# Two graph-attention layers in fp8 and bf16: products that read the weights' three parts in place

## The reference

```python
def _L0_gnn_ref(h, adj, a):
    src, dst = h @ a[:D, 0], h @ a[D:, 0]
    e = src[:, None] + dst[None, :]
    e = jnp.where(e > 0, e, 0.01 * e)
    e = jnp.where(adj > 0, e, NEG_INF)
    return jax.nn.softmax(e, axis=1) @ h
...
x = _layernorm(x + _L0_gnn_ref(x, adj, L0_gnn_a), axis=-1)
x = _layernorm(x + _L1_gnn_ref(x, adj, L1_gnn_W, L1_gnn_a), axis=-1)
```

## Time and profile before

| | |
|---|---|
| Median of 3 runs | 437.58 us (437.0 to 438.23) |
| The profiled execution's own time | 437.87 us |
| Its span, first to last instruction | 436.0 us |
| Mean granted TensorE clock | 0.992 |
| Busy: TensorE, weight loads | 406.4, 397.8 us |
| Busy: VectorE, ScalarE, GpSimd | 380.3, 382.9, 252.2 us |
| Chain that ended last | TensorE 75%, VectorE 15%, issue 6% |

### The profile page before, as it was taken

The page is one execution under the profiler, slowest core; times in us unless marked ns, Lnnn a source line. Parts: engine busy times, 40 slices in busy tenths (PEclk is TensorE's granted clock), DMA queues, the critical chain, the costliest instruction groups (busy, mean ns, idle before and its releaser), DMA issues.

```text
span 436.0 us, 11844 instructions
## 1 busy us (share of the span) xinstructions
PE 406.4 (93%) x4484; PEld 397.8 (91%) x4484; DVE 380.3 (87%) x683; ACT 382.9 (88%) x590; POOL 252.2 (58%) x292
## 2 busy tenths in 40 slices
PE   1599999999999999999999999999999999999980
PEld 1388999999999999999998998999999999999980
DVE  4799998899898989999889997689999999999963
ACT  3899986979979799779998989999999999999930
POOL 5533353753738547296493135568696969695931
PEclk9999999999999999999999999999999999999996
DMA  5999989799897998988610000000000000000000
GB/s 118 99 107 108 90 75 98 68 101 80 78 102 66 95 85 73 90 73 88 83 52 1 2 26 2 2 26 2 27 2 26 0 24 1 24 2 26 2 26 17
DMA packets 22766, 22.48 MB, mean 52 GB/s; under 512 B 1344, under 2 KB 22464, under 8 KB 22720
## 3 DMA queue, kind: packets, MB, share of 16 engines
q0 software_dynamic: 17424, 16.78, 44.4%
q1 hardware_dynamic: 4208, 4.05, 2.9%
q10 hardware_dynamic: 1088, 1.05, 0.7%
HBM read 69.30 MB, written 2.10 MB: 164 GB/s over the span
## 4 chain that ended last, share of the span: by engine, by line
PE 75%; DVE 15%; issue 6%; POOL 1%; DMA 1%; ACT 0%; DVEq 0%; POOLq 0%
PE acc L1223 67%; PE tb L1147 5%; DVE neg L831 3%; DVE pos L842 3%; DVE mask_t L757 2%; PE srcb L1157 1%; DMA mask_t<-in_x 1%; DVE split L814 1%; DVE mask_t L814 1%; PE pg L1191 1%; DVE scr L857 1%; DVE wmov L820 1%; DVE mask_t L913 1%; DVE dcol L921 1%; DVE enc L814 1%
## 5 line engine op out<-in xcount | busy, mean ns | idle before, releaser
L670 ACT ACTIVATE neg<-srcb,dcol 128x512 int8<-128x512 f32 x512 | 358.2, 973 | 4.4 <-PE acc L1223 4.0
L1223 PE MATMUL acc<-wmov,pos 128*128 128x195 bf16 x2016 | 357.1, 248 | 3.6 <-DVE pos L842 2.6
L1223 PE MATMUL acc<-wmov,neg 128*128 128x195 bf16 x2016 | 357.3, 249 | 0.0
L1223 PEld LDWEIGHTS acc<-wmov,pos 128*128 128x128 fp8e4 x2016 | 198.5, 98 | 7.6 <-DVE pos L842 5.6
L1223 PEld LDWEIGHTS acc<-wmov,neg 128*128 128x128 fp8e4 x2016 | 197.5, 98 | 2.3 <-issue 1.3
L842 DVE TENSOR_TENSOR pos<-neg,mask_t 128x1024 uint16<-128x1024 uint16 x128 | 104.8, 819 | 15.3 <-DVE neg L831 1.6
L831 DVE TENSOR_TENSOR neg<-neg,mask_t 128x1024 uint16<-128x1024 uint16 x128 | 102.9, 804 | 10.8 <-ACT neg L670 8.0
L490 POOL DMA_DIRECT2D enc<-in_adj x31 | 24.7, 798 | 63.5 <-DVE scr L857 31.1
L757 DVE TENSOR_SCALAR mask_t<-tb 128x512 uint32<-128x512 uint32 (+1 forms) x64 | 43.9, 686 | 6.7 <-PE tb L1147 6.0
L1147 PE MATMUL tb<-ident,enc 128*128 128x128 f32 x256 | 39.5, 278 | 2.7 <-DMA enc<-in_adj 2.7
L742 DVE SCALAR_TENSOR_TENSOR odd<-mask_t,odd 128x1024 uint32<-128x1024 uint32 x32 | 38.8, 1213 | 0.0
(11 more groups left out here) (139 smaller groups left out, 301.7 us busy)
## 6 DMA issues: line engine op xcount, KB each, us to landing
enc<-in_adj POOLq DMA_DIRECT2D x31, 512.0 KB, 8.2
mask_t<-in_x ACTq DMA_DIRECT2D x4, 256.0 KB, 5.7
x_rows<-xout SPq DMA_DIRECT2D x8, 128.0 KB, 3.1
resid<-x_rows SPq DMA_DIRECT2D x8, 128.0 KB, 2.1
out<-xout SPq DMA_DIRECT2D x8, 128.0 KB, 1.7
wmov<-mask_t SPq DMA_DIRECT2D x2, 390.0 KB, 3.4
enc<-in_adj POOLq DMA_DIRECT2D x2, 256.0 KB, 8.3
resid<-in_a SPq DMA_DIRECT2D x1, 64.0 KB, 4.6
```

Of the source, the lines that this page charges most:

```text
L670: ins = nc.scalar.activation(neg[:, k % SR, :, b], srcb[:, q % 2, :], ACT.Sign, bias=dcol[:, layer, c:c + 1])
L1223: ins = nc.tensor.matmul(acc[t][:, side * WC:(side + 1) * WC], m[:, t * P:(t + 1) * P, b], wmov[:, c, side * WC:(side + 1) * WC], start=fi ...
```

## The change

Every group gets a home of its own, 1,040 fp32 words: pairs of words (product, rest), side by side for each column. As bf16 these are four halves a column: the lower half of the product, its upper half, the lower half of the rest, its upper half. VectorE's second subtraction writes the rounded third part over the lower half of the rest, so halves 1, 2 and 3 of four are the three parts, and the moving operand reads them there, `halves_of(layer, g)[:, b, side, :, 1:4]`. `wmov`, `split`, the staged words, `keep_parts` and `move_weights` go. The accumulators hold the parts of a column side by side, 65 times 3, and the sums read them so. Layer 0's groups 0 and 1 lie in the mask's last supertile, the others in `wts`; layer 1's groups lie in `apart_wts`, in lots of `enc_lots` (the adjacency buffer, 16 words longer a lot) and in the first three lots of `wts`. Their writers wait for those homes to be free.

```diff
+        def home(layer, g):
+            if layer == 0 and g < TAIL:
+                flat = last_words[:, first_tail + g * LOT:first_tail + (g + 1) * LOT]
+            elif layer == 0:
+                flat = wts[:, g - TAIL]
+            else:
+                flat = {0: apart_wts[:, :], 1: enc_lots[:, 0], 2: enc_lots[:, 1], 3: wts[:, 0], 4: wts[:, 1],
+                        5: wts[:, 2], 6: enc_lots[:, 2], 7: enc_lots[:, 3]}[g]
+            return flat
+        def wait_for_home(eng, g):
+            if g in (1, 2, 6, 7):
+                lot = {1: 0, 2: 1, 6: 2, 7: 3}[g]
+                eng.wait_ge(turned, KB * (NQ - 1) + KP * (lot + 1))
+            elif g:
+                eng.wait_ge(mm_done, KB * (NQ - 1) + g)
+        def parts_of(layer, g):
+            return home(layer, g).rearrange("p (b s c r) -> p b s c r", b=NB, s=2, r=2)
+        def halves_of(layer, g):
+            return home(layer, g).bitcast(BF16).rearrange("p (b s c h) -> p b s c h", b=NB, s=2, h=4)
+        def moving(layer, g, b, side):
+            return halves_of(layer, g)[:, b, side, :, 1:4]
...
 def multiply(eng, ops, layer, g):
-            if n > 1:
-                eng.wait_ge(w_vec, WEIGH * (n - 1))
-                eng.wait_ge(w_act, n - 1)
-            ops.tensor_tensor(parts_of(layer, g)[:, :, :, 0, :], ...
+            ops.tensor_tensor(parts_of(layer, g)[:, :, :, :, 0], ...
...
 gpsimd, layer 0, supertile 6:
-                    groups = {3: (0,), 5: (1,)}
+                    groups = {3: (0,), 7: (1,)}
 gpsimd, change_layers:
-                w = wmov[:, NB * 7:NB * 8].rearrange("p b (s c) -> p b s c", s=2)[:, :, :, 0:2 * FD]
-                pool.wait_ge(w_vec, WEIGH * (NQ + 7) + 1)
-                nc.gpsimd.tensor_copy(w, top_of(1, 7).rearrange("p b s r c -> p b s (r c)")).then_inc(w_pool, 1)
...
 scalar:
-                nc.scalar.copy(w, top_of(layer, g).rearrange("p b s r c -> p b s (r c)")).then_inc(w_act, 1)
...
 extract, last supertile of layer 0:
-                            dve.wait_ge(moved[g], 16)
+                            dve.wait_ge(mm_done, KB * (NQ - 1) + g + 1)
...
 weigh:
-                nc.vector.tensor_tensor(rest, both[:, :, :, 0, :], top[:, :, :, 0, :], ALU.subtract)\
+                nc.vector.tensor_tensor(rest, product, halves[:, :, :, :, 1], ALU.subtract).then_inc(w_vec, 1)
-                nc.vector.tensor_tensor(w[:, :, :, 2, :], rest, top[:, :, :, 1, :], ALU.subtract)\
+                nc.vector.tensor_tensor(halves[:, :, :, :, 2], rest, halves[:, :, :, :, 3], ALU.subtract)\
...
 vector, layer 0, supertile 7:
+                        if k == 2:
+                            weigh(1, 1)
-                        if k >= STAGED + 2:
+                        if k >= 4:
                             weigh(1, k - 2)
 vector, layer 0, supertile 6:
-                        if k in (4, 6):
-                            weigh(1, k // 2 - 2)
+                        if k == 5:
+                            weigh(1, 0)
...
 tensor, products and one_tile:
-                                acc[t][:, side * WC:(side + 1) * WC], m[:, t * P:(t + 1) * P, b],
-                                wmov[:, c, side * WC:(side + 1) * WC], start=first, stop=last, skip_group_check=True)
+                                acc[t][:, side * WC:(side + 1) * WC].rearrange("p (c r) -> p c r", r=SPLIT),
+                            m[:, t * P:(t + 1) * P, b],
+                                moving(layer, k, b, side), start=first, stop=last, skip_group_check=True)
```

More of the change, by code:

```diff
@@ L31 @@
 EARLY = 5
-STAGED = 2
+TAIL = 2
+LOT = NB * 2 * FD * 2
 LOOKS = (4, 5, 6)
@@ L86, in fast_attention @@
         ident = sb("ident", [P, P], F32)
-        ones = sb("ones", [P, 1], F32)
-        share = sb("share", [P, 1], F32)
+        single = sb("single", [P, 3], F32)
+        ones, share, strange = (single[:, i:i + 1] for i in range(3))
         att1 = sb("att1", [F, 2], F32)
@@ L167, in fast_attention @@
         a_set = sem("a_set")
-        w_prod = [sem(f"w_prod{i}") for i in range(2)]
+        w_prod = sem("w_prod")
         w_vec = sem("w_vec")
-        w_act = sem("w_act")
-        w_pool = sem("w_pool")
         limits = sem("limits")
@@ L236, in weights_of @@
[L236 to L248, removed]
+        first_tail = KB * TI * P - TAIL * LOT
@@ L685, in body @@
                             exps_of_d(0, 0, KB * NB, 0)
-                        else:
-                            keep_parts(0, k - 1)
                         if k == 6:
                             exps_of_s(0, 0, 2)
-                    if layer == 0 and is_second(q) and k == 0:
-                        keep_parts(0, KB - 1)
                     if layer == 0 and is_second(q) and k == KB - 1:
@@ L748, in extract @@
                 if is_last(q):
-                    if k == 0:
-                        dve.wait_ge(w_act, NQ + STAGED)
-                    for g in range(STAGED):
-                        if k == steps_of(g)[0]:
-                            dve.wait_ge(moved[g], 16)
+                    for g in range(TAIL):
+                        if k == (first_tail + g * LOT) // (TI * P):
+                            dve.wait_ge(mm_done, KB * (NQ - 1) + g + 1)
                 apart(dve, q)
@@ L808, in weigh @@
                 n = NQ * layer + g
-                both, top = parts_of(layer, g), top_of(layer, g)
-                rest = both[:, :, :, 1, :]
-                w = weights_of(layer, g).rearrange("p b (s r c) -> p b s r c", s=2, r=SPLIT)
-                dve.wait_ge(w_prod[g % 2], n // 2 + 1)
-                nc.vector.tensor_tensor(rest, both[:, :, :, 0, :], top[:, :, :, 0, :], ALU.subtract)\
-                    .then_inc(w_vec, 1)
-                if layer == 1 and not is_staged(1, g):
-                    dve.wait_ge(mm_done, KB * (NQ - 1) + g + 1)
+                both, halves = parts_of(layer, g), halves_of(layer, g)
+                product, rest = both[:, :, :, :, 0], both[:, :, :, :, 1]
+                dve.wait_ge(w_prod, n + 1)
+                nc.vector.tensor_tensor(rest, product, halves[:, :, :, :, 1], ALU.subtract).then_inc(w_vec, 1)
                 dve.wait_ge(w_vec, WEIGH * n + 1)
-                nc.vector.tensor_tensor(w[:, :, :, 2, :], rest, top[:, :, :, 1, :], ALU.subtract)\
+                nc.vector.tensor_tensor(halves[:, :, :, :, 2], rest, halves[:, :, :, :, 3], ALU.subtract)\
                     .then_inc(w_vec, 1)
@@ L1236, in one_tile @@
                         ins = nc.tensor.matmul(
-                            acc[t][:, side * WC:(side + 1) * WC], m[:, t * P:(t + 1) * P, b],
-                            wmov[:, c, side * WC:(side + 1) * WC], start=False, stop=last, skip_group_check=True)
+                            acc[t][:, side * WC:(side + 1) * WC].rearrange("p (c r) -> p c r", r=SPLIT),
+                            m[:, t * P:(t + 1) * P, b],
+                            moving(1, k, b, side), start=False, stop=last, skip_group_check=True)
                 return ins
```

76 lines of the change are left out of this document (14 added, 62 removed).

## The result

| | before | changed |
|---|---|---|
| Median | 437.29 us (436.97 to 438.23) | 536.0 us (535.92 to 536.28) |
| Ratio, 95% interval | | 1.2248 (1.2219 to 1.2276) |
| Span of the profiled execution | 436.0 us | 534.7 us |

The account below looks back on a forecast made before the run. TensorE's products were taken to bound most of the kernel, with VectorE level in the first supertile and ahead of TensorE's waits at the layer change. Terms 0 + 0 - 0.6 + 0.2 + 0 = -0.4 us gave 437.2 us, range 434.5 to 441.5.

Parts of the forecast that it names:

- (a): TensorE's products reading runs of three halves: 86.5 ns each, unchanged, chosen over the other end, 114.1 ns.
- Rival 2: TensorE's moving port passes 4-byte words: 114.1 ns a product, +113 us, 550 us in all; chance 0.10.
- Term (b): VectorE's subtractions on words 8 bytes apart: 0.70 us each, unchanged; range of the pair +0 to +1.0 us.
- rival 1: VectorE's subtractions, first supertile and layer change, pay for 8-byte steps: +0.5 us each, +13 us, 450 us; chance 0.10.
- up to 0.9 ns: Loss per element of a VectorE operation in 8-byte steps by the skill page's rule; estimated 0.5 us for 520.
- Term (c): GpSimd's products writing in 8-byte steps: 1.07 us each, taken as 0 change, up to +2.7 us if held up.
- ScalarE's copies and SyncE's moves at 0: Removing ScalarE's 15 copies of parts and SyncE's two moves of staged weights gains 0 us.
- GpSimd's copy at -0.6: Removing GpSimd's last-group copy, which slowed VectorE's second subtraction before step 7's masks in the layer change: -0.6 us.
- the moved subtractions at +0.2: Second group's two VectorE subtractions move from supertile 6 to step 2 of supertile 7: +0.2 us, between 0 and +1.4.
- Rivals 3 and 4: 3: smaller cost at layer change or in GpSimd's products, 440 us, 0.12; 4: layer change gains more, 435.3 us, chance 0.23.

Follow-up runs that it names:

- the padded kernel: Kernel before, one half of padding after each side's 195 weights, so positive-side reads begin at multiples of 16 bytes: 435.21 us against 437.16, ratio 0.9949.
- the run with whole words: Changed kernel, but products read only halves 2 and 3 of four (98 pairs), leaving out the product's upper half: 449.88 us, ratio 1.0287.
- the run with a whole-word write: Changed kernel, second subtraction writing fp32 over the rest's whole word, products reading only the two upper halves of each column: 442.77 us, ratio 1.013.

## Why the prediction was wrong

**The term that failed** is (a), "Products ... I take 86.5". It measured 111.8. The argument for it, that weight loads read single bytes 4 bytes apart faster than a word-wide port could, was sound against a port that passes words, and the step of 4 bytes shows that the moving port is none either (88.6 ns for 195 words). It said nothing about runs, and the layout of the change was not single halves but runs of three. In their place the runs showed 130 accesses for 195 columns where one piece needs 98. Both ends were in the sum; choosing between them by a row of another port was the mistake, and a chance of 0.10 for 4,096-fold work with no row of its own was too small.

**Rival 2** (550 us, 114.1 ns) had the place and nearly the size for a wrong reason, by luck: it counted 130 words at 0.85 ns, and 130 is also 65 runs of two accesses each, at 0.83. What the runs show is a cost per odd run: against a positive product of the padded kernel (83.4 ns), a positive one of the change takes 26.6 ns more over 65 runs, **0.41 ns a run, one column at 2.4 GHz**; runs of five (100.0 ns) 16.6 over 39, 0.43. Two columns of a run go together, and the last of an odd run takes the place of two: 32 accesses more than one piece are 26.7 ns. This is inferred from paces; no row shows the port.

**Term (b)**, subtractions at 0.70 us, was half right. The first stayed at 0.70 with all its steps at 8 bytes; the second went to 1.32, for its 2-byte results 8 bytes apart. So rival 1 had one operation of two. Its price could be seen only with the products mended: 7.1 us between the run with whole words (449.88) and the run with a whole-word write (442.77), where one operation of two at 13 / 2 = 6.5 us was rival 1's own figure.

The Trainium skill's "Vector Engine (DVE) Microarchitecture Reference", section "Measured stream behaviour on trn2", would have slowed every operand in steps of 8 bytes; for fp32 words this trace disagrees (0.69 to 0.70 us for 520, reads and write alike). The prediction's "up to 0.9 ns" is its row for all three streams hopping; its row for steps of 24 words is dearer, so it was no upper bound. The Trainium skill's "SBUF — State Buffer", section "Door 1: The DMA port swizzle", with its two hits in 16 bytes, would leave both the runs of three (six hits) and the step of 8 bytes (two) at full pace on TensorE; they take 111 and 176 ns. At 16 bytes, one hit, the pace halves again, but it had halved at the step before too: what agrees is the line of 16 bytes as the unit that costs, not the two hits as a threshold.

**Term (c)**, GpSimd's products at 1.07 us, held (minimum 1.062, median 1.07 to 1.08 in the changed kernel).

**ScalarE's copies and SyncE's moves at 0, GpSimd's copy at -0.6 and the moved subtractions at +0.2**, a sum of -0.4 us: with the prices of (a) and (b) out of the way the rest is -0.3 us by the whole-word write. That is a difference of medians with about 0.7 us of interval either way, and behind products that are 1.4 ns slower, so it supports that the rest is small, not each term. ScalarE's busy time fell only by 3.8 us, not by 15: its copies went (590 instructions to 575), but its overlapping signs spread out when they wait for products (the mean of one is down from 973 to 846 ns, yet 365.5 us are busy against 358.2).

**Rivals 3 and 4** found no support. Waits in the change of layers fell behind slow products; with the whole-word write, the nearest to the old pace, weight loads wait 4.2 us for masks there (213 to 260 us) against 3.9 before.

**The method.** I called the products' pace the thing that would prove me wrong first, "0.3 ns on each is already 1.3 us". That was the right place to look and should have set the range.

## What to carry to other kernels

Where one instruction form fills the bound engine, an edit of how it reads its operand is the largest term of the change, however much work is saved elsewhere: measure that read by itself first, with one edit of the access pattern and garbage for values. On TensorE's moving operand of bf16 keep runs even and steps at 4 bytes or less, begin reads at multiples of 16 bytes and, by the count above that no run of its own tests, let no pair cross one: padding that costs 128 bytes a partition gave 2 us here. Parts of a number that lie inside wider words are cheap to make but are read and written (2 bytes in 8) at up to twice the price.

## What the runs showed of the hardware that I had not expected

| moving operand, bf16 | columns | ns a product |
|---|---|---|
| one piece, from a multiple of 16 bytes | 195 or 196 | 83.4 |
| one piece, from elsewhere (8 bytes off among others) | 195 or 196 | 86.7 to 87.4 |
| runs of 4, pitch 6 halves, from multiples of 8 bytes | 196 | 84.2 |
| runs of 4, pitch 5 | 196 | 94.2 |
| runs of 2, pitch 4, either start | 196 | 88.6 |
| single halves, 4 bytes apart | 195 | 88.6 to 89.4 |
| runs of 5, pitch 6 | 195 | 100.0 |
| runs of 3, pitch 4, three starts | 195 | 110.9 to 113.3 |
| single halves, 8 bytes apart | 195 | 176.3 |
| single halves, 16 bytes apart (granted clock 0.528) | 195 | 345.7 |

The last entry holds at 2.4 GHz too, as its piece across both levels shows. Its granted clock fell at 81.9 us although products stood 346 ns apart without a gap before that, and stayed at the lower level but for 3.4 us, with TensorE busy for 1504.3 of the 1530.5 us.

One more number: the first products of every run start more slowly. Leaving out the first distance, the 16 of the first group start 163.3 ns apart before and 163.4 in the change, the pace of 195 columns at 1.2 GHz (162.5). The trace records the granted clock only from 22.5 us on before and from 24.3 in the change (windows ahead of that read 1.00 for want of a record), and at 24.38 us the distances there fall from 162 to 110 ns. So at the lower level odd runs cost nothing that can be seen, while a step of 8 bytes takes its 176 ns there too. The access of 0.83 ns and the line of 1.8 ns thus seem to keep a rate of their own, which the array's slower pace hides. That was not tested further, nor were other types than bf16.
